# Other orders, another split between VectorE and ScalarE, and routing in steps of eight, in a fused attention and expert kernel

## The chip, the core and the metric

The kernel runs on one core of a Trainium2 chip. Its engines work from queues of their own and meet at semaphores: TensorE (PE; its weight loads are PEld), VectorE (DVE), ScalarE (ACT), GpSimd (POOL), and SyncE (SP), which issues most DMAs. The metric is the device time in microseconds (us) of one execution. An execution also comes with the clock that TensorE was granted.

## The reference

A block of 16 sequences of 512 tokens, 128 features wide. Layer-normed tokens go through an attention of 16 heads of 64 and, apart from that, through a mixture of 8 experts, of which a router picks 2 for each token. Everything is float32.

```
xn = layernorm(x)                              # x: 16 x 512 x 128
h = rmsnorm(xn) * norm_scale
q, k, v = h @ wq, h @ wk, h @ wv               # 16 heads of 64
attn = (softmax(q k^T / 8) v) @ w_out + b_out
logits = silu(xn @ rw1 + rb1) @ rw2 + rb2      # 128 -> 512 -> 8
p, e = softmax of the top 2 of logits, and which they are
ffn = sum over the 2 of p * (silu(xn @ w1[e] + b1[e]) @ w2[e] + b2[e])
out = x + attn + ffn
```

## The kernel before

The program is written out by hand as one list per engine. The work is cut into 256 steps (`group(G)`, G from 0 to 255; the sequence is `b = G // 16`, and `g = G % 16` the step in it), and six more that drain it. Two steps make a pair of heads `n = G // 2`: an even step and an odd one.

What a step of attention holds. It makes the scores of two of the pair's four row blocks (`scores`, S0 and S1, line 396, two PSUM banks each). VectorE takes the negated maxima (`maxima`, line 405) and ScalarE the exponentials (`probs`, line 411, four a step). It transposes the probabilities of the step before (`turn_probs`, T0 and T1, line 426, two banks each), and ScalarE or VectorE copies them out of PSUM (lines 438 and 441: `TURN_ON`, by row block, says who). It projects keys or queries of the next pair ("kq", `project`, line 240; ScalarE rounds them at 380, VectorE makes the rest at 381). An odd step ends with `weighted` (line 455, 16 matmuls, and OT on VectorE at 461). Steps with `g % 4 == 2` add `project_out` (lines 501 and 503), and steps with `g` in 0, 4, 8 and 12 make two value tiles (`values`; `VALUES_ON` says who copies them out, lines 361 and 363).

What goes beside it. First comes the router, in blocks of seven steps, one block for each sequence (`route`; `h = G % 7` is the step in the block). At `h` 0 and 2 `router` does two of four chunks each: 3 matmuls, two ScalarE activations (557, 560) and two POOL operations. `logits` is at 5 and `turn_logits` at 6. In the next block's `h` 0, `choose` picks the two experts in some 20 small VectorE operations, each waiting for the last (parts 0, 1 and 2: lines 615 to 620, 622 to 628, 632 to 635), with a tanh on ScalarE (629) that waits for line 628. `place` at `h` 1 works out where the tokens go, and `scatter` writes them to `slots` in HBM from POOL. After the last block `counting` writes the padding (`pads`) and has SP fetch the first rows.

Then come the experts, as 39 tiles of 512 token rows, one every three steps from step FIRST = 126 (`PLAN`: the keys are steps from `FIRST + 3 * i`). For a tile: `fetch_rows` (716) has SP load its rows, `turn_rows` transposes them (line 745) and splits them (ScalarE 750, VectorE 751); `expert_in` (h) does four chunks of 3 matmuls, each followed by two ScalarE activations (763, 765); `expert_halves` combines them on VectorE (774), rounds the sum (`HIGH_ON`, by chunk: ScalarE 777 or VectorE 779) and makes the rest on POOL (780). `expert_out` (y) does 12 matmuls (788 to 790) and ScalarE adds the bias (794); `give_back` transposes (803) and scales (807); `add_rows` has POOL add the rows to the output with four indirect DMAs (815), each lot after the landing of the lot before. Before the core ends, `again` loads the last sequence's rows from the output once all expert rows are added, and `finish` adds the last attention sum (527) and stores it (531).

What sets the order. Within a step, PE goes through the parts in the order of `PE_ORDER` (row 0 for even steps, row 1 for odd). VectorE and ScalarE sort what the step gave them by `DVE_ORDER` and `ACT_ORDER` (lines 36 to 43), where work without a place of its own is "side". POOL and SP take it as it comes. In an even step turn0 and turn1 are the copies of row blocks 2 and 3, in an odd step those of 0 and 1. All engines work in order, so an instruction that waits holds up everything behind it on its engine.

The eight PSUM banks are handed out while the list is written, by a small model with a work time and a hold time for each kind (`HOLD`, `take`): each request gets the bank that the model expects to be free first. The matmuls then wait for the operation that really empties that bank.

## Time and profile before

| | |
|---|---|
| median of 3 runs | 2053.0 us (2047.12, 2053.0, 2056.13) |
| the profiled execution's own time | 2047.12 us |
| its span, first to last instruction | 2045.3 us |
| mean granted clock | 0.989 |
| PE, PEld busy | 1955.3 us (96%), 1257.6 us (61%) |
| DVE, ACT, POOL busy | 1624.6 us (79%), 1506.4 us (74%), 930.1 us (45%) |

PE is busy 96% of the span, but matmuls are pipelined and their ends modelled, so this is no measure of how full it is. The row of starts tells more: back to back, a matmul of 512 columns starts 0.23 us after the last. The other engines have idle time on the average. Averages hide that the program has two long stages of equal step count, routing and experts, and what they are bound by has to be read stage by stage.

### The profile page before, as it was taken

To read this page: it belongs to the slowest core of one execution; us is meant where nothing else is said; L and a number is where in the kernel's file an instruction comes from. 1 tells how busy PE (TensorE), PEld (TensorE's weight loads), DVE (VectorE), ACT (ScalarE), POOL (GpSimd) and SP (SyncE) were. 2 spreads that over 40 slices of the span, in tenths; PEclk is the share of its full clock that TensorE was granted. 3 is DMA by queue.
4 is the path that set the end of the run, shared out by engine and by line. 5 is a ranking of instruction groups with operands and counts; after the bars stand their busy time and mean duration, and the time that the engine had idled before them with its cause. 6 is when DMAs were issued, how large, how long until landed. Compare 5 with 4: busy or idle time off the path is not lost.

```text
span 2045.3 us, 45195 instructions
## 1 busy us (share of the span) xinstructions
PE 1955.3 (96%) x16646; PEld 1257.6 (61%) x16646; DVE 1624.6 (79%) x2798; ACT 1506.4 (74%) x3572; POOL 930.1 (45%) x794
## 2 busy tenths in 40 slices
PE   7999999989999999989999999999999999999998
PEld 5656555556555555556666666666666666666664
DVE  7878788888888887877777777777777877777786
ACT  5767676767666666656878788888787888887865
POOL 4435364654444444310364554644645546446430
PEclk9999999999999999999999999999999999999999
DMA  2113222321111111113243333433433434334220
GB/s 84 36 56 105 80 93 75 107 77 40 40 38 38 38 43 33 34 48 93 71 79 92 80 79 89 85 85 79 84 86 79 88 81 89 88 79 84 58 37 28
DMA packets 132761, 142.22 MB, mean 70 GB/s; under 512 B 25486, under 2 KB 99086, under 8 KB 132494
## 3 DMA queue, kind: packets, MB, share of 16 engines
q1 hardware_dynamic: 101374, 118.34, 18.4%
q0 software_dynamic: 31168, 20.99, 9.0%
q8 instruction: 134, 2.20, 0.5%
q14 instruction: 85, 0.70, 0.1%
HBM read 102.92 MB, written 38.72 MB: 69 GB/s over the span
## 4 chain that ended last, share of the span: by engine, by line
PE 72%; DVE 11%; ACT 9%; issue 4%; POOL 1%; DMA 1%; another core or an unknown queue 0%; SPq 0%; DVEq 0%; ACTq 0%; POOLq 0%
PE pair L455 20%; PE pair L396 15%; PE pair L426 10%; PE pair L240 6%; PE pair L242 4%; PE pair L241 4%; DVE NM L405 4%; ACT PR L411 3%; PE pair L501 2%; PE pair L503 2%; DVE PT L441 2%; PE pair L788 1%; PE pair L790 1%; PE pair L789 1%; ACT ZT L763 1%
## 5 line engine op out<-in xcount | busy, mean ns | idle before, releaser
L411 ACT ACTIVATE PR<-pair,NM 128x512 f32<-128x512 f32 x1024 | 710.9, 717 | 30.6 <-DVE NM L405 28.0
L405 DVE TENSOR_REDUCE NM<-pair 128x2 f32<-128x1024 f32 x512 | 611.5, 1210 | 44.8 <-PE pair L396 34.8
L438 ACT COPY PT<-pair 128x512 f32<-128x512 f32 x512 | 277.2, 599 | 396.4 <-PE pair L426 395.8
L396 PE MATMUL pair<-KS,QS 64*128 64x512 f32 x3072 | 489.2, 422 | 25.9 <-ACT HS L560 10.3
L455 PE MATMUL pair<-PT,V 128*64 128x512 f32 x2048 | 474.6, 606 | 2.1 <-ACT PR L411 2.0
L426 PEld LDWEIGHTS pair<-idn,PR 64*128 64x128 f32 x8192 | 336.9, 139 | 103.9 <-ACT HS L560 22.8
L780 POOL TENSOR_TENSOR HH<-ZZ,HH 128x512 fp32r<-128x512 f32 x156 | 201.4, 1355 | 413.6 <-ACT HH L777 413.6
L396 PEld LDWEIGHTS pair<-KS,QS 64*128 64x128 f32 x3072 | 256.0, 187 | 194.2 <-issue 141.5
L426 PE MATMUL pair<-idn,PR 64*128 64x64 f32 x8192 | 343.5, 223 | 21.4 <-ACT HS L560 16.4
L441 DVE COPY PT<-pair 128x512 f32<-128x512 f32 x512 | 327.1, 680 | 8.0 <-remote 5.1
L455 PEld LDWEIGHTS pair<-PT,V 128*64 128x64 f32 x2048 | 137.1, 138 | 263.0 <-issue 248.5
L815 POOL DMA_INDIRECT out<-YS,IDW x156 | 250.1, 1603 | 60.8 <-issue 42.0
L411 ACT ACTIVATION_READ_ACCUMULATOR PR<-pair,NM 128x1 f32 x1024 | 237.7, 232 | 0.0
L461 DVE TENSOR_TENSOR OT<-pair,RB 128x512 f32<-128x512 f32 x128 | 88.4, 691 | 164.9 <-PE pair L455 160.4
L563 POOL TENSOR_TENSOR TH<-TH,HS 128x512 f32<-128x512 f32 x64 | 81.9, 1280 | 265.8 <-ACT HS L560 265.7
L774 DVE SCALAR_TENSOR_TENSOR ZZ<-ZT,ZZ 128x512 f32<-128x512 f32 x156 | 112.2, 721 | 92.2 <-ACT ZZ L765 92.2
L666 POOL DMA_INDIRECT slots<-XR,IDX x128 | 125.7, 982 | 84.6 <-DVE junk L662 53.9
L763 ACT ACTIVATE ZT<-pair,BT 128x512 f32<-128x512 f32 x156 | 114.7, 735 | 2.5 <-DVE ZZ L774 1.3
L765 ACT ACTIVATE ZZ<-pair,BT 128x512 f32<-128x512 f32 x156 | 115.6, 741 | 0.0
L381 DVE TENSOR_TENSOR QS<-pair,QS 128x512 fp32r<-128x512 f32 x128 | 87.3, 682 | 15.4 <-ACT QS L380 15.1
L381 DVE TENSOR_TENSOR KS<-pair,KS 128x512 fp32r<-128x512 f32 x128 | 87.3, 682 | 8.9 <-ACT KS L380 8.9
L777 ACT CAST HH<-ZZ 128x512 fp32r<-128x512 f32 x117 | 71.5, 674 | 23.9 <-DVE ZZ L774 23.9
(168 smaller groups left out, 2831.6 us busy)
## 6 DMA issues: line engine op xcount, KB each, us to landing
E<-w_tab SPq DMA_DIRECT2D x78, 512.0 KB
RB<-l_rows SPq DMA_DIRECT2D x127, 256.0 KB
XG<-slots SPq DMA_DIRECT2D x39, 264.0 KB
w_tab<-SPL SPq DMA_DIRECT2D x16, 512.0 KB
l_rows<-RT SPq DMA_DIRECT2D x508, 1.0 KB
xin<-in_x SPq DMA_DIRECT2D x16, 256.0 KB, 7.7
XQ<-in_x SPq DMA_DIRECT2D x16, 256.0 KB, 7.4
RAW<-in_w SPq DMA_DIRECT2D x16, 256.0 KB
```

The lines of the kernel that those rows point to most:

```text
L381: add("dve", lambda e: e.tensor_tensor(lo, bank[bk], hi, ALU.subtract), needs=[(name + "hi", n), *old], name=(name + "lo", n), place="low")
L396: m = e.matmul(bank[bk + j], a[half[j], cols], c[half[j], :], start=(k == 0), stop=(k == 2))
L405: add("dve", lambda e: e.tensor_reduce(NM[:, 2 * t:2 * t + 2], both[:], AX.X, ALU.max, negate=True), needs=[("S", n, t), *([("exp", n - 1, ...
L411: add("act", lambda e: e.activation(PR[:, k, :], bank[bk], ACT.Exp, bias=NM[:, k:k + 1], accum_out=RS[:, n % 2, j, t:t + 1]), needs=[("max ...
L426: m = e.transpose(bank[two[r]][:, at:at + DH], PR[rows, 2 * t + j, c * P:(c + 1) * P], idn[rows, rows])
L438: add("act", lambda e, r=r: e.copy(dst[r], src[r]), needs=[("T", n, t), *old], name=("PT", n, t, r), place=f"turn{t % 2}")
L441: add("dve", lambda e, r=r: e.tensor_copy(dst[r], src[r]), needs=[("T", n, t), *old], name=("PT", n, t, r), place=f"turn{t % 2}")
L455: m = e.matmul(bank[bk][j * DH:(j + 1) * DH, :], V[:, k, h * DH:(h + 1) * DH], PT[:, n % 2 * 2 + j, k, :], start=(k == 0), stop=(k == QT - 1))
L666: add("pool", lambda e, k=k, t=t: e.indirect_dma_start(slots, bass.IndirectOffsetOnAxis(ap=IDX[:, r % 2, k, t:t + 1], axis=0), XR[:, r % 2 ...
L763: add("act", lambda e: e.activation(ZT[:, n % 2], bank[bk], ACT.Tanh, bias=BT[:, i % 2, 8 + c:9 + c], scale=0.5), needs=[("h1", i, c), ("b ...
L780: add("pool", lambda e: e.tensor_tensor(lo, ZZ[:, r], hi, ALU.subtract), needs=[("hi", n), old], name=("lo", n))
L815: add("pool", lambda e, t=t: e.indirect_dma_start(out, bass.IndirectOffsetOnAxis(ap=IDW[:, i % 4, t, 0:1].bitcast(U32), axis=0), YS[:, i % ...
```

## The change

It moves work in the three tables that say who does what: one copy of row block 1's transposed probabilities a pair goes from VectorE to ScalarE (`TURN_ON`), two value copies a sequence too (`VALUES_ON`), and the rounding of expert chunks 0 and 1 goes from ScalarE to VectorE (`HIGH_ON`). The routing block gets eight steps in place of seven, so that `h` 0 is always an even step; `choose` part 0 moves to `h` 7 of the block before, and `turn_x` to `h` 7. The experts start at step 138 in place of 126. In `PLAN` the rows are fetched 2 steps before their transposes in place of 5, the transposes stand in the step of the tile before and ahead of its matmuls, and the last chunk's halves come a step earlier; the last tile hands back its rows two steps earlier than the others. The order tables and the bank model's hold times are other ones. Much of the order tables is without effect: `weighted` does nothing in even steps, `sums` and `values` have nothing in odd ones.

```diff
 PE_ORDER = [
-    "S0 weighted T0 S1 T1 kq spread attend inverse experts ahead route".split(),
-    "ahead S0 T0 S1 spread T1 kq route attend experts inverse weighted".split(),
+    "S0 T0 S1 T1 inverse kq spread attend ahead weighted experts route".split(),
+    "S0 T0 S1 spread T1 kq ahead attend experts route inverse weighted".split(),
 ]
 DVE_ORDER = [
-    "inverse max0 max1 turn1 turn0 low values sums side".split(),
-    "sums values max0 max1 turn1 low turn0 side inverse".split(),
+    "inverse max0 turn0 max1 turn1 low values sums side".split(),
+    "max0 turn0 max1 inverse turn1 sums values low side".split(),
 ]
 ACT_ORDER = [
-    "turn0 exp00 exp01 turn1 high exp10 exp11 values side hi".split(),
-    "turn0 exp00 exp01 high turn1 values exp10 exp11 side hi".split(),
+    "turn0 exp00 exp01 turn1 high exp10 exp11 values hi side".split(),
+    "turn0 exp00 exp01 high values turn1 exp10 exp11 hi side".split(),
 ]
-TURN_ON = [["act", "act"], ["dve", "dve"], ["act", "act"], ["dve", "dve"]]
-VALUES_ON = [["dve", "act", "dve", "act"], ["act", "dve", "act", "dve"]]
-HIGH_ON = ["act", "act", "dve", "act"]
+TURN_ON = [["act", "act"], ["dve", "act"], ["act", "act"], ["dve", "dve"]]
+VALUES_ON = [["dve", "act", "act", "act"], ["dve", "act", "act", "act"]]
+HIGH_ON = ["dve", "dve", "dve", "act"]
 PLAN = {
-    -7: [("rows",)],
-    -3: [("in",)],
-    -2: [("turn",)],
-    0: [("h", 0), ("halves", 0), ("h", 1), ("halves", 1), ("h", 2), ("halves", 2), ("out",), ("h", 3)],
-    2: [("halves", 3)],
+    -5: [("rows",)],
+    -3: [("turn",), ("in",)],
+    0: [("out",), ("h", 0), ("halves", 0), ("h", 1), ("halves", 1), ("h", 2), ("halves", 2), ("h", 3)],
+    1: [("halves", 3)],
     3: [("y",)],
     5: [("back",), ("add", 0), ("add", 1)],
 }
-OWN = {0: {-1: [("turn",)]}}
+OWN = {0: {-1: [("turn",)]}, -1: {2: [("y",)], 3: [("back",), ("add", 0), ("add", 1)]}}
 HOLD = {
-    "S0": (0.9, 5.2), "S1": (0.7, 6.5), "T": (0.5, 3.1), "kq": (0.8, 1.5), "V": (0.8, 2.2), "PV": (3.6, 1.4),
+    "S0": (0.9, 4.6), "S1": (0.7, 6.2), "T": (0.5, 2.5), "kq": (0.8, 1.8), "V": (0.8, 2.2), "PV": (3.6, 1.7),
...
-    ROUTE = 7
-    EARLY = ROUTE * NB // GB
-    FIRST = ROUTE * NB + 14
+    EARLY = NB // 2
+    FIRST = EARLY * GB + 10
...
         def route(G):
-            r, h = divmod(G, ROUTE)
+            r, h = divmod(G, 8)
             if 0 < r <= NB:
                 if h == 0:
-                    choose(r - 1, 0)
                     choose(r - 1, 1)
                     choose(r - 1, 2)
                 if h == 1:
                     place(r - 1)
-                if 2 <= h <= 4:
+                if r == NB:
+                    if h == 2:
+                        scatter(r - 1, slice(0, 8))
+                elif 2 <= h <= 4:
                     scatter(r - 1, slice(3 * h - 6, 3 * h - 3))
...
+            if h == 7:
+                choose(r, 0)
             if r + 1 < NB:
...
-                if h == 6:
+                if h == 7:
                     turn_x(r + 1)
 
         def counting(G):
-            k = G - ROUTE * NB
+            k = G - 8 * NB
             if k == 2:
                 totals()
-            if 6 <= k < 10:
-                pads(2 * k - 12)
-                pads(2 * k - 11)
-            if k == 7:
+            if 4 <= k < 8:
+                pads(2 * k - 8)
+                pads(2 * k - 7)
+            if k == 5:
                 fetch_weights(0, 0)
+            if k == 6:
+                fetch_weights(0, 1)
             if k == 8:
-                fetch_weights(0, 1)
-            if k == 10:
                 fetch_rows(0)
                 fetch_rows(1)
```

The first place is VectorE's queue where the router's choice stands. In the kernel before, this is the end of an even step at `h` 0: KS is the key rest, acc the output sum, gm and gt hold the choice.

```order
L381 TENSOR_TENSOR KS<-pair1,KS 128x512 [waits s_act_khi]
L510 TENSOR_TENSOR acc<-pair3,acc 128x512 [waits s_dve_acc,s_pe_OP]
L615 TENSOR_REDUCE gm<-LG 128x4 [waits s_dve_gate]
L616 TENSOR_TENSOR gt<-LG,gm 128x32 [waits s_dve_gate]
L617 SCALAR_TENSOR_TENSOR gt<-gt,CON 128x32 [waits s_dve_gate]
L618 TENSOR_REDUCE gm<-gt 128x4 [waits s_dve_gate]
L619 TENSOR_TENSOR gt<-CON,gm 128x32 [waits s_dve_gate]
L620 SCALAR_TENSOR_TENSOR gt<-gt,LG 128x32 [waits s_dve_gate]
```

Thirteen more small operations of `choose` follow, and then the next step's first maxima. In the changed kernel part 0 stands at the end of the odd step before (lines after the edit are two lower):

```order
L379 TENSOR_TENSOR QS<-pair0,QS 128x512 [waits s_act_qhi]
L613 TENSOR_REDUCE gm<-LG 128x4 [waits s_dve_gate]
L614 TENSOR_TENSOR gt<-LG,gm 128x32 [waits s_dve_gate]
L615 SCALAR_TENSOR_TENSOR gt<-gt,CON 128x32 [waits s_dve_gate]
L616 TENSOR_REDUCE gm<-gt 128x4 [waits s_dve_gate]
L617 TENSOR_TENSOR gt<-CON,gm 128x32 [waits s_dve_gate]
L618 SCALAR_TENSOR_TENSOR gt<-gt,LG 128x32 [waits s_dve_gate]
L344 TENSOR_TENSOR XT<-pair3,XT 128x512 [waits s_pe_r1,s_act_xTs]
L459 TENSOR_TENSOR OT<-pair1,RB 128x512 [waits s_RB_0,s_pe_PV]
L464 RECIPROCAL RI<-RS 128x8 [waits s_dve_rt,s_act_exp]
L467 STREAM_TRANSPOSE RT<-RI 128x32 [waits s_rrow_1,s_dve_ri]
L403 TENSOR_REDUCE NM<-pair0 128x2 [waits s_pe_S]
```

and parts 1 and 2 stay at the end of the even step, ahead of the next step's first maxima (NM):

```order
L379 TENSOR_TENSOR KS<-pair1,KS 128x512 [waits s_act_khi]
L620 TENSOR_REDUCE gm<-gt 128x4 [waits s_dve_gate]
L621 TENSOR_TENSOR gt<-gt,gm 128x32 [waits s_dve_gate]
L622 SCALAR_TENSOR_TENSOR gt<-gt,CON 128x32 [waits s_dve_gate]
L623 TENSOR_REDUCE gm<-gt 128x4 [waits s_dve_gate]
L624 TENSOR_TENSOR gt<-CON,gm 128x32 [waits s_dve_gate]
L625 TENSOR_TENSOR gt<-gt 128x32 [waits s_dve_gate]
L626 TENSOR_TENSOR gm<-gm 128x4 [waits s_dve_gate]
L630 TENSOR_TENSOR PM<-PM,gt 128x8 [waits s_dve_pm] x4
L633 COPY PM<-PM 128x8 [waits s_dve_pm]
L403 TENSOR_REDUCE NM<-pair1 128x2 [waits s_pe_S]
```

Six of the operations have moved one step ahead; the others still stand before the maxima.

The second place is ScalarE's queue in an even step that carries an expert tile's matmuls. The kernel before (V is a value copy, ZT and ZZ the activations of the four chunks, YT the bias of the tile before, HH the rounding, PT the next step's first copies; pair0 to pair3 are the bank pairs):

```order
L361 COPY V<-pair2 128x512 [waits s_pe_V]
L763 ACTIVATE ZT<-pair3,BT 128x512 [waits s_bt_0,s_pe_h1]
L765 ACTIVATE ZZ<-pair3,BT 128x512 [waits s_pool_lo]
L763 ACTIVATE ZT<-pair0,BT 128x512 [waits s_pe_h1]
L765 ACTIVATE ZZ<-pair0,BT 128x512 [waits s_pool_lo]
L763 ACTIVATE ZT<-pair2,BT 128x512 [waits s_dve_s,s_pe_h1]
L765 ACTIVATE ZZ<-pair2,BT 128x512 [waits s_pool_lo]
L763 ACTIVATE ZT<-pair0,BT 128x512 [waits s_dve_s,s_pe_h1]
L765 ACTIVATE ZZ<-pair0,BT 128x512 [waits s_pool_lo]
L794 ACTIVATE YT<-pair2,BT 128x512 [waits s_pe_yT,s_pe_w2]
L777 CAST HH<-ZZ 128x512 x2
L438 COPY PT<-pair3 128x8x64 [waits s_pe_PV,s_pe_T]
```

The changed kernel, in the same place:

```order
L359 COPY V<-pair3 128x512 [waits s_pe_V]
L748 CAST X2<-pair3 128x512 [waits s_pe_h1,s_pe_xg]
L761 ACTIVATE ZT<-pair0,BT 128x512 [waits s_bt_0]
L763 ACTIVATE ZZ<-pair0,BT 128x512 [waits s_pool_lo]
L761 ACTIVATE ZT<-pair1,BT 128x512
L763 ACTIVATE ZZ<-pair1,BT 128x512 [waits s_pool_lo]
L761 ACTIVATE ZT<-pair1,BT 128x512 [waits s_dve_s]
L763 ACTIVATE ZZ<-pair1,BT 128x512 [waits s_pool_lo]
L761 ACTIVATE ZT<-pair0,BT 128x512 [waits s_dve_s]
L763 ACTIVATE ZZ<-pair0,BT 128x512 [waits s_pool_lo]
L792 ACTIVATE YT<-pair3,BT 128x512 [waits s_pe_yT,s_pe_w2]
L436 COPY PT<-pair3 128x8x64 [waits s_pe_PV,s_pe_T]
```

The cast of the next tile's rows (X2), which waits for the last `expert_in` matmul (s_pe_h1), now stands ahead of all eight activations, and the two roundings behind them are gone.

On PE, this is what follows the tile's last `expert_out` matmul in such a step (E2 is the second weight, PR the probabilities). It reads like this in both kernels; only the second signal that T0's bank waits for differs:

```order
L788 MATMUL pair2<-HH,E2 128x512
L394 MATMUL pair3<-KS,QS 128x512 [waits s_act_exp]
L394 MATMUL pair3<-KS,QS 128x512 x5
L424 MATMUL pair1<-idn,PR 128x64 [waits s_act_zz,s_dve_xl]
L424 MATMUL pair1<-idn,PR 128x64 x15
L394 MATMUL pair0<-KS,QS 128x512 [waits s_act_zz]
L394 MATMUL pair0<-KS,QS 128x512 x5
L424 MATMUL pair2<-idn,PR 128x64 [waits s_act_ye]
L424 MATMUL pair2<-idn,PR 128x64 x15
```

The second transposes T1 (the last two rows) go into the bank that YT empties (s_act_ye).

The third place is VectorE's queue in such a step. Before:

```order
L381 TENSOR_TENSOR KS<-pair3,KS 128x512 [waits s_act_khi]
L510 TENSOR_TENSOR acc<-pair0,acc 128x512 [waits s_dve_acc,s_pe_OP]
L774 SCALAR_TENSOR_TENSOR ZZ<-ZT,ZZ 128x512 [waits s_act_zz,s_act_zt] x3
L779 CAST HH<-ZZ 128x512 [waits s_pe_w2,s_dve_s]
L405 TENSOR_REDUCE NM<-pair2 128x2 [waits s_pe_S]
L405 TENSOR_REDUCE NM<-pair3 128x2 [waits s_pe_S]
L441 COPY PT<-pair1 128x8x64 [waits s_pe_T]
```

and after the change:

```order
L379 TENSOR_TENSOR KS<-pair1,KS 128x512 [waits s_act_khi]
L749 TENSOR_TENSOR X2<-pair3,X2 128x512 [waits s_pe_h1,s_act_xh]
L772 SCALAR_TENSOR_TENSOR ZZ<-ZT,ZZ 128x512 [waits s_act_zz,s_act_zt]
L777 CAST HH<-ZZ 128x512 [waits s_pe_w2,s_dve_s]
L772 SCALAR_TENSOR_TENSOR ZZ<-ZT,ZZ 128x512 [waits s_act_zz,s_act_zt]
L777 CAST HH<-ZZ 128x512 [waits s_dve_s]
L772 SCALAR_TENSOR_TENSOR ZZ<-ZT,ZZ 128x512 [waits s_act_zz,s_act_zt]
L777 CAST HH<-ZZ 128x512 [waits s_dve_s]
L403 TENSOR_REDUCE NM<-pair2 128x2 [waits s_pe_S]
```

The three sums (ZZ) stood together with one rounding behind them; now each has its rounding (HH) behind it, and X2 stands ahead, all before the next step's maxima.

## Rows read from the trace of the kernel before

**Rows 1.** Stretches, routing then experts: length, busy PE, PEld, DVE, ACT, POOL, clock, DMA, GB/s.
```profile
16.70:861.90 845.20, 789.23 (x6950) 488.72 (x6950) 695.84 (x1420) 583.87 (x1438) 395.80 (x375) 0.98 0.17 57
...
979.80:1924.90 945.10, 936.13 (x7682) 623.83 (x7680) 737.18 (x1065) 764.12 (x1742) 484.62 (x372) 1.00 0.38 83
```
**Rows 2.** The first stretch, line 396 alone: length, PE, PEld, clock, DMA, GB/s.
```profile
16.70:861.90 845.20, 213.47 (x1344) 111.24 (x1344) 0.98 0.17 57
```
**Rows 3.** Timeline of three late steps: start, length, engine, instruction.
```profile
1996.50 0.96 PE L396 MATMUL pair<-KS,QS 64*128 64x512 f32 x6
...
2001.73 0.96 PE L396 MATMUL pair<-KS,QS 64*128 64x512 f32 x6
...
2008.83 0.96 PE L396 MATMUL pair<-KS,QS 64*128 64x512 f32 x6
```
**Rows 4.** Timeline of step 43, odd, at h 1, and its neighbours.
```profile
338.42 0.18 DVE L615 TENSOR_REDUCE gm<-LG 128x4 f32<-128x32 f32 x1
...
339.09 0.96 PE L396 MATMUL pair<-KS,QS 64*128 64x512 f32 x6
...
342.38 0.20 ACT L629 ACTIVATE gm<-gm 128x4 f32<-128x4 f32 x1 [3.66 <-DVE gm L628]
...
345.04 1.12 PE L426 MATMUL pair<-idn,PR 64*128 64x64 f32 x16 [3.75 <-ACT HS L560]
...
352.78 0.97 PE L396 MATMUL pair<-KS,QS 64*128 64x512 f32 x6
```
**Rows 5.** The costliest copies, from the page's groups: busy, mean ns.
```profile
L438 ACT COPY PT<-pair 128x512 f32<-128x512 f32 x512 | 277.2, 599 | 396.4 <-PE pair L426 395.8
...
L441 DVE COPY PT<-pair 128x512 f32<-128x512 f32 x512 | 327.1, 680 | 8.0 <-remote 5.1
```
**Rows 6.** Timeline of step 174, even, with an expert tile, on PE and ACT.
```profile
1374.79 0.39 PE L242 MATMUL pair<-X,E 128*128 128x512 f32 x1
...
1377.59 0.40 PE L790 MATMUL pair<-HH,E 128*128 128x512 f32 x1
1377.92 0.96 PE L396 MATMUL pair<-KS,QS 64*128 64x512 f32 x6
...
1379.96 0.65 PE L426 MATMUL pair<-idn,PR 64*128 64x64 f32 x16
```
**Rows 7.** The same step's activations on ACT, first and last.
```profile
1373.13 0.69 ACT L763 ACTIVATE ZT<-pair,BT 128x512 f32<-128x512 f32 x1
...
1377.13 0.73 ACT L765 ACTIVATE ZZ<-pair,BT 128x512 f32<-128x512 f32 x1
```
**Rows 8.** Lines 774 and 779 alone: shortest, median and longest ns.
```profile
L774 DVE SCALAR_TENSOR_TENSOR ZZ<-ZT,ZZ x156: 677/692/1725, 969.9 to 1948.9; 128x512 f32<-128x512 f32 x156
...
L779 DVE CAST HH<-ZZ x39: 426/428/703, 973.0 to 1935.9; 128x512 fp32r<-128x512 f32 x39
```
**Rows 9.** Timeline of step 150, DVE and POOL: three sums beside POOL's work.
```profile
1171.21 3.48 DVE L774 SCALAR_TENSOR_TENSOR ZZ<-ZT,ZZ 128x512 f32<-128x512 f32 x3 [1.23 <-ACT ZZ L765]
1171.83 1.71 POOL L780 TENSOR_TENSOR HH<-ZZ,HH 128x512 fp32r<-128x512 f32 x1
```
**Rows 10.** Timelines before the first expert tile: SP issue, POOL's first use, PE's first.
```profile
943.76 1.61 SPq L716 DMA_DIRECT2D XG<-slots  x2
...
950.57 0.19 POOL L754 COPY IDW<-XG 128x8 f32<-128x8 f32 x1 [61.19 <-DMA XG<-slots]
...
958.40 0.60 PE L745 MATMUL pair<-idn,XG 128*128 128x128 f32 x4
```
**Rows 11.** The last steps' timeline: the reload of the last rows, the last addition.
```profile
2024.06 0.43 SPq L1017 DMA_DIRECT2D xin<-out  x1
...
2041.44 0.69 DVE L527 TENSOR_TENSOR xin<-pair,xin 128x512 f32<-128x512 f32 x1 [0.75 <-PE pair L519]
```
**Rows 12.** DMA issues by line: size, us from issue to landing.
```profile
xin<-out SPq DMA_DIRECT2D x1, 256.0 KB, 7.6
```
**Rows 13.** Line 815 alone, the indirect adds: shortest, median, longest ns.
```profile
L815 POOL DMA_INDIRECT out<-YS,IDW x156: 1546/1562/2045, 1011.7 to 1989.3; - x156
```

4 rows, old and new, of the table HOLD are left out of this document.

## Prediction

> **What bounds the kernel now.** I read the busy time by stretch first, because averages over the span mix two stages. Steps 0 to 111 take 845.2 us (7.55 a step) and steps 128 to 239 take 945.1 (8.44) [rows 1]; each holds 112 steps, 1344 score matmuls at twelve a step [rows 2]. In the expert stretch PE is busy 936.1 of 945.1 us at a granted clock of 1.00, in the routing stretch 789.2 of 845.2 at 0.98. So the expert stage is full of matmuls, and a wait there adds to the time almost one for one, while there is nothing to win. The routing stage has 56 us without a matmul, which is all that an edit can win.
>
> The timeline says where these 56 us lie. Attention alone makes a pair of steps in 12.33 us (1996.50 to 2008.83), 5.23 even and 7.10 odd [rows 3]. Step 43, odd and at `h` 1, takes 13.69 us (339.09 to 352.78) [rows 4]. There `choose` holds up VectorE from 338.42, ScalarE's tanh waits 3.66 for its line 628, the router's activations stand behind the tanh, and the T1 transposes wait 3.75 for the bank that the router's HS (line 560) empties. With blocks of seven, `h` 1 is odd in every second block.
>
> **A, the routing stage.** An odd step with router work and without a stall I put at 7.7 (7.10 and 0.6 for the router's matmuls), so the stall of step 43 is 6.0. Seven such steps lie in the stage; 37 us (5.3 each, a little under step 43, since 7 x 6.0 = 42 would leave too little of the 56 for the rest) is what they can give. With blocks of eight, `h` 0 is always even and `choose` in all 16 blocks stands before an odd step. Six of its 20 operations move to the odd step before. Up to line 628 there are 13, which took 3.96 (338.42 to 342.38, [rows 4]), 0.30 each; without six the tanh comes 1.8 sooner. So the wait is about halved and not gone: ScalarE's tanh, the activations behind it and with them T1's bank still come late. VectorE also loses a copy of 680 ns a pair [rows 5]. Of the 3.75 that T1 waited [rows 4], 1.8 and 0.7 go, which leaves 1.3 in each of 16 odd steps, 21 us. A = -37 + 21 = -16. Bounds: -37 if the shorter `choose` is hidden; +5 if the copy doesn't help, because ScalarE now makes it (599 ns [rows 5]) just ahead of the late activations, and 2.6 a block remain (3.75 - 1.8 + 0.6; 16 x 2.6 = 42).
>
> **B, the expert stage.** The rows of PE in the change show that T1 goes into the bank of YT. Now the X2 cast, which waits for the tile's last `expert_in` matmul, stands ahead of all eight activations. In step 174 that matmul starts at 1374.79 and ends at 1375.18, the last of `expert_out` ends at 1377.99, and T1 starts at 1379.96 [rows 6]. The eight activations started at 1373.13, the last at 1377.13, 0.57 apart [rows 7]: they ran beside the matmuls, and YT was due when `expert_out` ended. In the new order the same step runs so: the cast starts at about 1375.3 and takes some 0.6, the eight activations end at 1375.9 + 8 x 0.57 + 0.15 = 1380.6, YT at about 1381.1. T1, wanted at 1379.96, waits 1.1. Of the 39 tiles 20 start in an even step; in 19 of these T1 has this bank.
>
> VectorE comes on top. Its three sums now wait for activations that are done later, each with a rounding of 0.43 behind it in place of one for all [rows 8], and POOL's line 780 (1.71) falls between them. Beside POOL's work the sum of 692 ns grew to as much as 1725 [rows 8]; in step 150 three of them took 3.48 in place of 2.1 [rows 9]. The Trainium skill, "SBUF — State Buffer", section "Who interferes with whom", says that a VectorE operation with two inputs in SBUF, or a copy or cast in a two-port mode, excludes a GpSimd operation that uses the shared pair for as long as either runs. The trace agrees as far as the sums go (1725 against 692), and by that rule the roundings would be drawn in as well. The longest rounding of before took 703 against 428 [rows 8]. With the last sum due at 1380.6 at the earliest and 0.69 + 0.43 behind it, the next step's maxima start near 1383 and not near 1381, and exponentials and the odd step's banks follow. I put this at 0 to 0.9 more. Per even tile 1.1 to 2.0, and 1.4 as my value, nearer to 1.1, because that end stands on rows alone: 20 x 1.4 = 28 us.
>
> In the 19 odd tile steps the 16 matmuls of `weighted` (3.65 us or so) follow the expert matmuls and hide most of it; there I put 0.2 each, 4 us. B = +32. Bounds: +5, if ScalarE makes up for the cast in the slack between YT and T1 (1.4 us in rows 6, from 1377.99 plus YT's 0.6 to 1379.96), and +60 at 2.6 an even tile and 0.4 an odd one.
>
> **C, the changeover.** SP fetched the first rows at 943.76, POOL used them at 950.57, and PE at 958.40 [rows 10], a slack of 7.83 us. PE now uses them one step after the fetch and not three, so two steps (a pair, 12.33) are gone: 12.3 - 7.8 = 4.5, and PE waits about 5 us, once. Bounds 0 and 8. In later tiles the fetch is 2 steps, near 17 us, before the transposes; the first one needed 6.8 from issue to use (943.76 to 950.57), so these cost nothing. C = +5.
>
> **D, the tail.** Before, the last rows were reloaded at 2024.06, and the last sum started at 2041.44 [rows 11]; the reload takes 7.6 [rows 12], so it was 9.8 early. The four adds of the last tile now come in step 255, which starts near 2026.4 (2008.83 + 12.33 + 5.23, [rows 3]). From about 2027 they take 6.2 to issue (4 x 1.56, [rows 13]) and two landings, for which no row stands and I allow 2 each; the reload then starts at 2037.5 and lands at 2045, 4 late, and I take 5 with the hand-back before them. Bounds 0 and +12.
>
> The moves of equal price (the order tables' other entries, `turn_x` at `h` 7, the split of VectorE's and ScalarE's copies outside the places above) I put at nothing: what hides them is the idle time of VectorE and ScalarE in the expert stretch (945.1 less 737 and less 764, [rows 1]). With that cover gone they would cost what B's upper bound holds.
>
> **The sum.** -16 + 32 + 5 + 5 = +26. The profiled execution took 2047.1 in all; that makes 2073. The median of the three is 5.9 above it. I take half of that, and come to 2076. What can be told from no change is 0.5%, about 10 us to either side of 2053 (2043 to 2063).
>
> **The rivals.**
> *R1, the orders do little (near 2053).* T1's wait in the even tile steps is 1.1 or less with no part of VectorE's, and the routing stage gives 25: -25 + 15 + 10 = 0 from 2053. For it: DVE and ACT are busy at most 81% of the expert stretch [rows 1], and lateness of one step can be made up for in the next two. Against it: a wait of PE in a stage in which PE is 99% busy isn't made up for.
> *R2, faster (near 2025).* The routing stalls go entirely (-37), the clock there rises from 0.98 to 1.00 with them, and YT comes before T1; with 10 for C and D that is 2026. It decides at the point where YT ends against T1's start: if the activations of chunks 0 to 2 get ahead of the cast's wait, or `expert_in` ends 1.1 us earlier in the step, nothing is left of B. For it: 56 us are there. Against it: the order of the rows of ScalarE.
> *R3, slower by much (near 2095).* PE's pauses in the expert stage bring its clock down, as in the routing stage, where the mean granted clock is 0.98 with stalls of this kind and 1.00 without them [rows 1]. 2% of 945 is 19 us more: 2076 + 19 = 2095. The Trainium skill, "TensorE: Matmul & The Clock Gate", section "A second HAM failure mode: psum-queue depth-cycling", describes a kernel whose small idle times between groups of matmuls, cycling through PSUM banks, made the clock swing between its levels. Here the stage with the short waits alone shows 1.00, and only the one with stalls of several us shows less, which speaks for the rule's effect only if the new waits are longer than 1 to 2 us.
>
> **Chances.** The forecast 0.50, of which 0.03 lies within 0.5%; R1 0.20 (0.12 same, 0.04 slower, 0.04 faster); R3 0.16, slower; R2 0.14, faster. Together slower 0.67, same 0.15, faster 0.18. The forecast's own range is 2060 to 2092. The range for 8 in 10 leaves R2's core out, and reaches over R1 and most of R3: 2038 to 2110, which also holds the sum with B at 5 (2049) and at 60 (2104).
>
> **What would show it.** A: in the routing stage, waits of T1 (now line 424) on HS in all odd steps after `choose`, about 1.3 and not 3.75, and the stage's steps at 7.4 (7.55 before). B: in even tile steps ScalarE idle before the X2 cast, T1 waiting about 1 us for YT some 19 times, lines 772 and 777 longer than 692 and 428 ns, steps at 8.7 (8.44 before). C: one wait of PE on XG of about 5. D: a sum at the end that waits for the reload. I am wrong if T1 doesn't wait for YT, or if the expert stage still takes 8.44 a step.

## The result and the profile after

The changed kernel took 2102.1 us (median of four, 2101.68 to 2103.31) against 2052.9 (2047.12 to 2056.13): 1.0244 of the time before, 95% interval 1.0221 to 1.0267. That is 49 us slower where 23 were forecast (2076 against 2053). Its profiled execution took 2104.14 with a span of 2102.3, 57 us over the span of before, of which the forecast's sum had explained 26.

Stretches of the changed kernel: steps 0 to 111, the changeover 128 to 137, the expert steps 138 to 254 (columns as in [rows 1]).

```profile
17.10:829.00 811.90, 767.45 (x6892) 475.66 (x6892) 643.94 (x1285) 604.32 (x1489) 354.57 (x337) 1.00 0.18 57
...
948.00:1033.65 85.65, 69.58 (x596) 43.53 (x594) 55.37 (x103) 48.46 (x122) 10.13 (x12) 0.88 0.24 70
...
1033.65:2074.30 1040.65, 990.90 (x8006) 655.76 (x8004) 819.03 (x1114) 793.29 (x1813) 519.71 (x381) 0.99 0.35 77
```

Steps 0 to 111 fell from 845.2 to 811.9, partly because they hold 14 routing blocks and no longer 16. The expert steps take 8.89 each and PE has 50 us without a matmul in these 117 steps, where it had 9 in the 112 steps of 945.1 us [rows 1]. To compare kernels whose stages have other lengths, I take step starts from the starts of the first score matmul, and from each stage the attention alone, 6.17 us a step (half of 12.33, [rows 3]). What is left is the stage's excess. Routing is steps 0 to 111 (before) or 0 to 127 (changed), the gap reaches from there to the first tile, and the experts' column begins with the first tile and ends 120 steps later, which is when the last tile's rows go back, or at step 255 where the core's steps end sooner (117 steps, in the runs with the changed routing). The tiles are means over tiles 2 to 35:

| run, with its edit | routing | gap to the first tile | experts | from step 255's start | even tile, odd tile (3 steps) |
|---|---|---|---|---|---|
| before | 154 | 14 | 269 | 20.7 | 24.29, 26.53 |
| changed | 141 | 24 | 319 | 28.0 | 26.07, 27.29 |
| e5 before, X2 ahead | 137* | 12 | 315 | 22.4 | 26.34, 26.78 |
| e6 before, chunks 0, 1 on VectorE | 137* | 11 | 331 | 20.7 | 27.02, 27.10 |
| e10 before, chunk 0 | 154 | 17 | 305 | 20.7 | 26.14, 26.63 |
| e11 before, chunk 1 | 155 | 16 | 268 | 22.3 | 24.20, 26.57 |
| e14 before, last halves earlier | 162 | 16 | 294 | 20.7 | 24.85, 27.31 |
| e1 changed, X2 back | 139 | 23 | 364 | 27.7 | 27.40, 28.65 |
| e2 changed, roundings back | 139 | 22 | 320 | 27.0 | 26.47, 26.85 |
| e3 changed, hold times back | 137 | 25 | 318 | 27.6 | 26.06, 27.22 |
| e4 changed, splits back | 150 | 22 | 321 | 26.9 | 26.16, 27.31 |
| e9 changed, X2 and roundings back | 137 | 24 | 305 | 27.1 | 24.79, 27.93 |
| e15 as e9, order tables back | 137 | 24 | 308 | 27.2 | 24.99, 27.99 |
| e13 as e9, whole plan back | 135 | 21 | 270 | 30.6 | 24.43, 26.70 |
| e7 before, routing changed | 120* | 20 | 259 | 30.9 | 24.10, 26.51 |
| e8 before, part 0 earlier | 111* | 10 | 267 | 22.4 | 24.18, 26.54 |
| e12 before, parts 0, 1 earlier | 159 | 15 | 270 | 20.7 | 24.30, 26.52 |
| e16 as e8, splits changed | 138 | 14 | 275 | 20.7 | 24.43, 26.70 |
| e17 as e8, tanh behind router | 144* | 9 | 267 | 22.4 | 24.18, 26.53 |

The starred runs come from two groups of runs in which the kernel before took 2027 and 2028 us and not 2051 to 2054; its untouched routing stage had 137 there (e5, e6) and not 154 (e10, e11). Ratios are always against before in the same group, and routing excesses are compared only within one group. So the change's 57 us by stage: routing -13, changeover +10, experts +50, the end +7, and +3 because the nine steps after the last tile, which had 3 less than the 6.17, are gone. Over the same 117 steps from the first tile the experts' excess rose from 264 to 319, by 55; before, the last tile's second matmuls and hand-back came in the three steps behind these, and 5 of the 269 with them.

The granted clock moves between stages. The trace has TensorE at its lower level (0.50, 1.2 GHz) for 37.5 us of the routing stage before and for 10.2 after, for 6.8 and 20.5 us of the changeover, and for 0 and 13.7 us of the same 117 expert steps. As the level is half of the other one, such a stretch can cost at most half its length. So the clock gave up to 14 us back in the routing stage, and took up to 7 in each of the other two.

PE's waits in the expert stage, changed kernel (total us, times, longest):

```profile
PE pair L424 <- ACT YT L792: 11.8, 15, 1.1
PE pair L394 <- DVE KS L379: 9.7, 10, 1.2
PE pair L394 <- ACT ZZ L763: 7.2, 5, 2.0
PE pair L453 <- ACT PR L409: 5.2, 4, 1.3
PE pair L424 <- DVE OT L459: 5.0, 3, 2.1
```

and of before, which had next to none:

```profile
PE pair L788 <- POOL HH L780: 3.5, 2, 1.8
PE pair L240 <- ACT PT L438: 3.1, 9, 0.7
PE pair L426 <- ACT PT L438: 1.8, 3, 0.6
```

Step 186 of the changed kernel, even, with a tile (the place of [rows 6, 7]):

```profile
1470.34 0.39 PE L240 MATMUL pair<-X,E 128*128 128x512 f32 x1
...
1470.82 0.59 ACT L748 CAST X<-pair 128x512 fp32r<-128x512 f32 x1 [2.90 <-PE pair L240]
1471.30 0.70 ACT L761 ACTIVATE ZT<-pair,BT 128x512 f32<-128x512 f32 x1
...
1474.15 1.65 POOL L778 TENSOR_TENSOR HH<-ZZ,HH 128x512 fp32r<-128x512 f32 x1 [4.91 <-DVE HH L777]
...
1474.70 1.39 DVE L777 CAST HH<-ZZ 128x512 fp32r<-128x512 f32 x1
...
1475.87 0.74 ACT L792 ACTIVATE YT<-pair,BT 128x512 f32<-128x512 f32 x1
...
1476.76 0.71 PE L424 MATMUL pair<-idn,PR 64*128 64x64 f32 x16 [0.77 <-ACT YT L792]
```

ScalarE stands idle for 2.90 until the last `expert_in` matmul, casts X2, and only then begins the eight activations, 0.57 apart; T1 waits for YT. A rounding beside POOL's subtraction takes 1.39 and not the 0.43 of [rows 8]. The changeover and the end:

```profile
1027.24 1.12 PE L743 MATMUL pair<-idn,XG 128*128 128x128 f32 x4 [4.88 <-DMA XG<-slots]
...
2091.41 0.66 PE L517 MATMUL pair<-idn,acc 128*128 128x128 f32 x4 [0.79 <-DVE acc L508]
2094.44 0.42 SPq L1019 DMA_DIRECT2D xin<-out  x1
2097.41 0.69 DVE L525 TENSOR_TENSOR xin<-pair,xin 128x512 f32<-128x512 f32 x1 [6.06 <-DMA xin<-out]
```

The last sum waits for the reload, 5.3 us after its transposes end (2092.07); before, the reload was issued 17 us ahead of the sum [rows 11].

### The profile page after: what moved, and what is told of

The parts are those of the page before. It is cut to its first block, busy times and chain, and to the rows that moved or that the text cites. A ratio compares the mean times of both kernels' runs of the same rounds, so it can differ in the third digit from the quotient of the medians.

```text
span 2102.3 us, 45192 instructions
## 1 busy us (share of the span) xinstructions
PE 1966.5 (94%) x16646; PEld 1261.2 (60%) x16646; DVE 1627.6 (77%) x2716; ACT 1541.4 (73%) x3654; POOL 945.3 (45%) x790
## 4 chain that ended last, share of the span: by engine, by line
PE 65%; ACT 13%; DVE 11%; issue 7%; DMA 1%; another core or an unknown queue 1%; POOL 0%; SPq 0%; DVEq 0%; POOLq 0%; ACTq 0%
PE pair L453 17%; PE pair L394 12%; PE pair L424 9%; PE pair L238 6%; PE pair L240 5%; PE pair L239 4%; ACT PR L409 4%; DVE NM L403 4%; DVE ZZ L772 2%; PE pair L499 2%; PE pair L501 2%; ACT PT L436 2%; ACT ZZ L763 1%; ACT HS L558 1%; DVE PT L439 1%
## 5 line engine op out<-in xcount | busy, mean ns | idle before, releaser
L436 ACT COPY PT<-pair 128x512 f32<-128x512 f32 x640 | 360.1, 612 | 362.7 <-PE pair L424 362.5
L424 PE MATMUL pair<-idn,PR 64*128 64x64 f32 x8192 | 345.9, 223 | 41.9 <-ACT HS L558 18.1
L778 POOL TENSOR_TENSOR HH<-ZZ,HH 128x512 fp32r<-128x512 f32 x156 | 225.9, 1490 | 325.2 <-DVE HH L777 168.3
L813 POOL DMA_INDIRECT out<-YS,IDW x156 | 244.6, 1568 | 176.1 <-DVE YS L805 118.7
L439 DVE COPY PT<-pair 128x512 f32<-128x512 f32 x384 | 251.1, 682 | 21.9 <-remote 16.4
L772 DVE SCALAR_TENSOR_TENSOR ZZ<-ZT,ZZ 128x512 f32<-128x512 f32 x156 | 120.0, 769 | 23.3 <-ACT ZZ L763 23.3
L777 DVE CAST HH<-ZZ 128x512 fp32r<-128x512 f32 x117 | 111.8, 955 | 13.1 <-PE pair L788 10.3
L749 DVE TENSOR_TENSOR X<-pair,X 128x512 fp32r<-128x512 f32 x39 | 27.0, 692 | 111.0 <-ACT X L748 107.6
```

The source lines that it names most:

```text
L424: m = e.transpose(bank[two[r]][:, at:at + DH], PR[rows, 2 * t + j, c * P:(c + 1) * P], idn[rows, rows])
L436: add("act", lambda e, r=r: e.copy(dst[r], src[r]), needs=[("T", n, t), *old], name=("PT", n, t, r), place=f"turn{t % 2}")
L439: add("dve", lambda e, r=r: e.tensor_copy(dst[r], src[r]), needs=[("T", n, t), *old], name=("PT", n, t, r), place=f"turn{t % 2}")
L772: add("dve", lambda e: e.scalar_tensor_tensor(ZZ[:, r], ZT[:, n % 2], 1.0, ZZ[:, r], ALU.add, ALU.mult), needs=[("zt", n), ("zz", n)], nam ...
L778: add("pool", lambda e: e.tensor_tensor(lo, ZZ[:, r], hi, ALU.subtract), needs=[("hi", n), old], name=("lo", n))
L813: add("pool", lambda e, t=t: e.indirect_dma_start(out, bass.IndirectOffsetOnAxis(ap=IDW[:, i % 4, t, 0:1].bitcast(U32), axis=0), YS[:, i % ...
```

## The experiments

**e1_turn**, the changed kernel with this entry of the plan set back (and `side` ahead of `hi` in `ACT_ORDER`, as in e2, e9, e13 and e15):

```diff
-    -3: [("turn",), ("in",)],
+    -3: [("in",)],
+    -2: [("turn",)],
```

> The changed kernel with one entry of its plan set back: the next tile's rows are transposed and split (X2) one step after the expert matmuls and not in their step ahead of them, so ScalarE's cast no longer stands ahead of the eight activations. The order table has the late roundings behind the side work again, which by itself moves nothing. Theory 1 (the cast makes the activations, YT and with it T1 late, and this is most of what the expert stage lost): the wait of T1 on YT, 1 us in the even tile steps, goes, the expert stage falls from 8.90 us a step to at most 8.6 and the time from 2102 to 2075 or less. Theory 2 (VectorE's three roundings beside POOL's work are most of it): 2092 to 2102, the waits on VectorE's KS and OT stay. Theory 3 (which bank each request gets is most of it): no firm number, since the banks are drawn anew, but the waits on ACT YT turn into waits on other signals of the same length, near 2095.

Measured 1.0453 (1.0432 to 1.0475), 45 us slower than the changed kernel. All three theories miss it. The waits on YT are nearly gone, but T1's place is taken by others: the scores wait 17.8 us for ZZ, and T1 16.6 for the copies. Something else makes ScalarE late when the cast doesn't.

**e2_high**: `HIGH_ON` back to act, act, dve, act.

> The changed kernel with the roundings of expert chunks 0 and 1 back on ScalarE (the order table as in the run beside it; by itself it moves nothing). Theory 1 (the cast ahead of the activations): nothing gained, 2095 to 2110, since ScalarE gets 1.2 us more a tile behind late activations. Theory 2 (roundings on VectorE, which POOL's port stretches from 0.43 to 0.95 us each): VectorE is 2 us a tile less busy, the waits of PE on KS, OT and on maxima go, and the time falls to 2080 or less. Theory 3 (banks): the banks are the same, so within 5 us of 2102.

1.0240 (1.0219 to 1.0261): no change, as theory 1 has it. While the cast is ahead, the roundings on VectorE cost nothing, stretched as they are.

**e3_hold**: the `HOLD` table of before.

> The changed kernel with the bank model's hold times of the kernel before, nothing else. Theories 1 and 2: every engine's queue but the choice of banks is the same, so the late activations and roundings stay and the time is 2095 to 2110. Theory 3 (the choice of banks is most of the loss): 2080 or less, with the waits of T1 on YT gone.

1.0212 (1.0195 to 1.0229), expert excess 318. The waits turn from YT to ZZ, and PE's time without a matmul stays (50 us, then 53). The bank model's hold times aren't the cause. Other hold times change only which bank each request gets, so that choice is tried as far as these two sets of times differ.

**e4_split**: `TURN_ON` and `VALUES_ON` of before.

> The changed kernel with the split of the probability copies and of the value copies between ScalarE and VectorE of before (one copy a pair and two value copies a sequence back on VectorE). Theory 1: ScalarE has 0.6 us a pair less in front of it, but VectorE 0.7 more; in the expert stage within 0.05 us a step, in the routing stage the choice comes 0.7 later, 16 x 0.3 = 5 us more: 2100 to 2110. Theory 2 (VectorE is what is late in the expert stage): 0.7 us more VectorE a pair beside the roundings costs 0.1 to 0.3 a step there, 2112 to 2130.

1.0311 (1.0293 to 1.0328). The new split was the one good part of these edits, worth 0.7%, in the profiled executions 9 us in the routing stage and 2 in the experts'. The time lies in theory 2's range, but not where that puts it; theory 1 had the place right and half the size.

**e5_b_turn**, the kernel before with the inverse of e1:

> The kernel before with one edit: the next tile's rows are transposed and split (X2) in the step of the tile before, ahead of its matmuls, so ScalarE's cast stands ahead of the eight activations. Theory 1 (the cast alone makes the expert stage slower): YT and T1 late in even tile steps as in the changed kernel, 20 x 1.1 to 1.8 us, 2053 becomes 2075 to 2090. Theory 2 (the roundings on VectorE are needed for it): within 10 us of 2053. Theory 3 (banks): anything between, with waits on other signals than YT.

1.0224 (1.0207 to 1.0241). This one line in the kernel before costs 46 us of expert excess, nearly all that the whole change lost there, 2.05 in each even tile. That is theory 1's cause, and more than its 1.8 a tile; but T1 waits for YT only 3.3 us in all, and S1 for the bank of ZZ 16.4, which was theory 3's sign. In both cases the bank comes free late because ScalarE's activations are late.

**e6_b_high**, the kernel before with `HIGH_ON` dve, dve, dve, act:

> The kernel before with one edit: expert chunks 0 and 1 are rounded on VectorE as well. Theory 1: VectorE has slack in the expert stage (633 us busy of 812), so within 10 us of 2053. Theory 2 (the roundings beside POOL's work on VectorE): the roundings take about 0.9 us each in place of 0.43, the maxima behind them come 1.8 later, and the time is 2070 to 2090.

1.0309 (1.0292 to 1.0326), 62 us of excess, more than either theory allows. Its step 174 shows a wait that I hadn't priced:

```profile
1381.42 0.43 DVE L779 CAST HH<-ZZ 128x512 fp32r<-128x512 f32 x1 [2.91 <-PE pair L790]
...
1382.48 1.37 DVE L779 CAST HH<-ZZ 128x512 fp32r<-128x512 f32 x1
1382.54 0.69 ACT L763 ACTIVATE ZT<-pair,BT 128x512 f32<-128x512 f32 x1 [2.52 <-DVE ZZ L774]
...
1384.53 0.96 PE L396 MATMUL pair<-KS,QS 64*128 64x512 f32 x6 [1.83 <-ACT YT L794]
```

The first rounding writes the buffer that the tile before is still being multiplied from, so it waits 2.91 for the last `expert_out` matmul. Behind it in VectorE's queue is the second sum, and chunk 3's tanh waits for that, 2.52. So the rounding makes the last activations as late as the cast does, by another way.

**e10_high_c0** and **e11_high_c1**, chunk 0 alone (dve, act, dve, act) and chunk 1 alone (act, dve, dve, act):

> The kernel before with chunk 0 alone rounded on VectorE besides chunk 2. The rounding stands behind the first sum and waits for the last expert_out matmul (its buffer's last reader), so the second sum and with it chunk 3's tanh wait. Theory 1 (this wait in VectorE's row is the cost): nearly the whole loss of the run with chunks 0 and 1, 1.024 to 1.03 of the time before. Theory 2 (the roundings beside POOL's subtractions on the shared port are the cost): half of that, 1.01 to 1.017.

> The kernel before with chunk 1 alone rounded on VectorE besides chunk 2: as many roundings beside POOL's work as in the run with chunk 0, but it stands behind the second sum, so chunk 3's tanh, which needs that sum, is free. Theory 1 (the wait that holds the second sum is the cost): ScalarE isn't held, only VectorE's third sum and the maxima are 1 us later: 1.000 to 1.008. Theory 2 (the port): as with chunk 0, 1.01 to 1.017.

1.0166 (1.0149 to 1.0183), and 1.0004 (0.9991 to 1.0017). The same operation, the same number of times, costs 36 us ahead of the second sum and nothing behind it. e10 lies in the range that I had given to the port, but its roundings aren't stretched (the median is 0.43 in both runs), and in e10 those of chunk 0 wait 81 us in all, ahead of the second sum. Those of chunk 1 in e11 wait 38 us, but behind the second sum, and no activation stands behind them. So the cost is the wait in that place. Both roundings together cost 26 more than chunk 0 alone; there those of chunks 1 and 2 take 1.37 and 1.39 (medians) beside POOL's subtractions:

```profile
L779 DVE CAST HH<-ZZ x117: 426/1372/1400, 950.4 to 1979.3; 128x512 fp32r<-128x512 f32 x117
```

```profile
L779 DVE CAST HH<-ZZ x78: 426/427/746, 974.4 to 1938.0; 128x512 fp32r<-128x512 f32 x78
```

(e6, then e11.) That the port is what these 26 are was not tried apart.

**e9_turn_high**: e1 and e2 together.

> The changed kernel with both edits set back: X2 is made a step after the expert matmuls, and chunks 0 and 1 are rounded on ScalarE. Theory 1 (the cast ahead of the activations, and the first rounding's wait on VectorE for the second matmuls of the tile before, each make the last activations about 2.5 us late in even tile steps, and together no later than one alone): only with both gone does the expert stage recover, from 8.89 us a step to 8.45 to 8.55, and the time is 1.000 to 1.006 of the kernel before. Theory 2 (orders, the rest of the plan, banks carry half of the loss): 8.7 a step, 1.012 or more.

1.0170 (1.0153 to 1.0187). Even tiles recover to 24.79, as theory 1 has it; odd tiles don't, at 27.93, so the time is theory 2's: another part of the change is at work. Of the 50 us, 36 are still there (305 against 269). With the cast back, the roundings on VectorE cost 59 (e1 against this run).

**e14_b_h3**, the kernel before with the last chunk's sum, rounding and rest a step earlier:

```diff
-    2: [("halves", 3)],
+    1: [("halves", 3)],
```

> The kernel before with one edit: the last chunk's sum, rounding and rest come one step after the tile's first step and not two. Theory 1: in odd tiles they then stand at the end of an even step, just ahead of the copies and maxima of the odd one, and ScalarE's rounding waits for VectorE's sum: 0.8 to 1.4 us in each of 19 odd tiles, 1.007 to 1.014. Theory 2 (this edit costs only beside the changed order tables): 0.997 to 1.003.

1.0099 (1.0074 to 1.0125): 24 us of expert excess, 0.78 an odd tile and 0.56 an even one. The 0.56 is nearly all in two even tiles (8 and 24), 3.8 us longer each: T1 waits 3.1 and 3.0 us for OT there, and as the wait ends TensorE falls to its lower level for 6.8 us. One of the two, then the stretch of low clock (columns as in [rows 1]):

```profile
1200.02 1.12 PE L426 MATMUL pair<-idn,PR 64*128 64x64 f32 x16 [3.10 <-DVE OT L461]
```

```profile
1199.60:1206.30 6.70, 6.28 (x31) 4.88 (x33) 5.45 (x10) 5.10 (x13) 1.28 (x1) 0.50 0.08 23
```

The odd tiles are regular. PE's wait and its cause in step 167:

```profile
1328.76 0.69 DVE L751 TENSOR_TENSOR X<-pair,X 128x512 fp32r<-128x512 f32 x1 [0.30 <-ACT X L750]
...
1329.37 0.91 DVE L774 SCALAR_TENSOR_TENSOR ZZ<-ZT,ZZ 128x512 f32<-128x512 f32 x1
...
1330.31 0.62 ACT L777 CAST HH<-ZZ 128x512 fp32r<-128x512 f32 x1 [1.58 <-DVE ZZ L774]
1330.84 1.07 ACT L438 COPY PT<-pair 128x512 f32<-128x512 f32 x2
...
1331.47 0.50 PE L240 MATMUL pair<-HT,WQ 128*128 128x512 f32 x1 [0.73 <-ACT PT L438]
```

The sum stands behind X2's rest, ScalarE holds the rounding 1.58 for it, and the copies that free the banks stand behind the rounding.

**e13_plan** and **e15_orders**: e9 with the whole plan of before, and e9 with its order tables.

> The changed kernel with ScalarE's roundings and the whole expert plan of before (the last chunk's halves two steps after the tile's first and not one, rows fetched five steps ahead); orders, splits, bank model and routing are the changed ones. With the transposes and roundings alone set back, even tiles recovered (24.8 us in three steps, 24.3 before) and odd ones did not (27.9 against 26.5), with PE waiting for ScalarE's copies behind the last chunk's rounding. Theory 1 (the last chunk's halves a step earlier): odd tiles fall to 26.5 to 26.8 and the time to 1.000 to 1.006 of before. Theory 2 (order tables or banks): odd tiles stay at 27.5 or more, 1.012 to 1.017.

> The changed kernel with X2, the roundings and the three order tables of before; the rest of the changed plan stays, with the last chunk's halves a step earlier. Theory 1 (that step is what odd tiles lose): 1.012 to 1.019, as without the tables. Theory 2 (the tables): odd tiles at 26.5 to 26.8, 1.000 to 1.006.

1.0008 (0.9999 to 1.0018), expert excess 270; and 1.0147 (1.0125 to 1.0170), excess 308. Setting back the plan and the roundings takes away 49 of the changed kernel's 319, setting back the order tables nothing. The plan was set back as a whole: beyond e9 that gives 35, where the halves alone cost 24 in the kernel before (e14). The halves alone were not tried in that kernel, so how much of the 35 is theirs, and how much comes from `out` ahead of the chunks, the later fetch or the splits beside them, stays open. e7 below has the same plan and blocks with the splits, tables and hold times of before, and 259 where e13 has 270.

**e7_b_route8** and **e8_b_choose**: before with the routing, changeover and first tile of the changed kernel; and before with the one edit

```diff
                 if h == 0:
-                    choose(r - 1, 0)
...
             if h == 6:
                 turn_logits(r)
+                choose(r, 0)
```

> The kernel before with the routing of the changed kernel and nothing else: blocks of eight steps, part 0 of the choice a step earlier, the scatter of the last block in one step, the experts from step 138. The routing stage should give 13 us (the excess over plain attention steps was 154 before and 141 in the changed kernel), the changeover should cost 10 (wait for the first rows, clock), the last tile's adds and the reload 7 to 10 at the end. Sum +4 to +7: 2053 to 2062. If the orders and splits of the changed kernel are needed for the routing gain, it is 2065 or more; if the end and the changeover cost less with the plan of before, 2045 or less.

> The kernel before with one edit: part 0 of the choice (six small VectorE operations) moves from the first step of a routing block to the last step of the block before. If the stall at the steps at h 1 is the length of the choice ahead of the maxima (13.7 us in step 43, where a step without it takes 7.7), 1.8 us go in each of the seven odd ones, 10 to 15 us in all: 2038 to 2043. If the stall is set by something else (the clock, the scatter, the tanh), within 5 us of 2053.

0.9991 (0.9981 to 1.0000) and 0.9889 (0.9872 to 0.9905). Blocks of eight together with part 0 give 17 us of routing and pay for it in the gap (8) and at the end (10); of the 10 in the experts' column 5 are the three steps that it has less. Part 0 alone gives 26 us of routing, twice what I expected: odd steps at `h` 1 fall from 13.4 (e5, e6; 13.1 in before) to 10.0. The stage in e5, whose routing is that of before, and in e8 (columns as in [rows 1]):

```profile
17.13:845.13 828.00, 789.58 (x6950) 489.98 (x6950) 694.36 (x1420) 584.58 (x1438) 395.67 (x375) 0.97 0.18 58
```

```profile
16.65:818.75 802.10, 774.92 (x6950) 482.84 (x6950) 695.43 (x1426) 586.04 (x1438) 396.18 (x375) 0.99 0.18 60
```

PE's time without a matmul falls from 38 to 27 us, by the 10 to 15 that I expected. The other 15 are matmul time: the same 6950 matmuls are busy 790 us and then 775, as TensorE is at its lower level for 44 us in e5 and 10 in e8. **e18_choose_again** repeated it:

> The kernel before with part 0 of the choice a step earlier, a second time, beside the run above on the same chip: 0.987 to 0.991 again if its gain doesn't depend on the chip, nearer to 0.994 if part of it came from the chip that ran it first, on which the kernel before took 2026.8 us.

0.9885 (0.9868 to 0.9902), again in a group where before took 2028. It wasn't run alone where before takes 2051 to 2054; e16, part 0 with the changed splits, has 138 us of routing there against 154. It is the fastest version here, faster than both kernels.

**e12_choose01** (parts 0 and 1), **e16_choose_split** (part 0 and the changed splits), **e17_late** (part 0, and `router` listed ahead of the rest of `choose` at `h` 0):

> The kernel before with parts 0 and 1 of the choice (13 operations and the tanh) in the last step of the block before. With part 0 alone moved, the time was 0.989 of before, and in step 43 T1 still waited 2.44 us for HS, with the tanh standing 2.32 for VectorE. If the tanh's wait is what is left, T1 waits under 0.5 there and the time is 0.978 to 0.985. If the wait only moves one step ahead (ScalarE then holds the tanh in the last step of the block), it is 0.986 to 0.995.

> The kernel before with part 0 of the choice a step earlier (0.989 of before by itself) and the changed split of the probability and value copies (one copy a pair and two value copies a sequence more on ScalarE). In the changed kernel this split was worth 0.7% (9 us of it in the routing stage). If that holds here: 0.982 to 0.988. If ScalarE is what is late in the expert stage of this one, it costs there what it gives in the routing stage: 0.989 to 0.995.

> The kernel before with part 0 of the choice a step earlier, and in the block's first step the router's two chunks listed ahead of the rest of the choice, so that on ScalarE the tanh stands behind the router's four activations and no longer in front of them; PE's and VectorE's queues are those of the run with part 0 alone moved. If the tanh's wait for VectorE is what keeps HS and T1's bank late (2.44 us in step 43), that wait goes, and the time is 0.975 to 0.985 of before. If VectorE's lateness with the maxima is what is left, it is within 0.004 of the run beside it.

e12: 1.0008 (0.9996 to 1.0020), outside both ranges: the stall moves a step ahead, the odd steps at `h` 0 now take 13.0. e16: 0.9923 (0.9900 to 0.9947), the second range: the splits cost 6 to 8 us in the experts' stage here. And e17: 1.0033 (1.0022 to 1.0043), against both expectations; step 43 tells why, e17 first and then e8:

```profile
339.06 1.30 POOL L565 TENSOR_TENSOR HS<-HS,TH 128x512 f32<-128x512 f32 x1
339.14 3.82 DVE L632 TENSOR_TENSOR PM<-PM,gt 128x8 f32<-128x8 f32 x4
...
340.33 1.27 POOL L563 TENSOR_TENSOR TH<-TH,HS 128x512 f32<-128x512 f32 x1
341.67 1.27 POOL L565 TENSOR_TENSOR HS<-HS,TH 128x512 f32<-128x512 f32 x1
```

```profile
328.19 0.76 DVE L632 TENSOR_TENSOR PM<-PM,gt 128x8 f32<-128x8 f32 x4
```

With the tanh behind the router's activations, POOL's operations on their results (1.3 each) start while VectorE is still in the choice, and four additions of eight columns take 3.82 and not 0.76. In the whole of e17, 22 of the 64 such additions take over 0.6 us, each while POOL works; in e8 and e18 none does.

## Why the prediction was wrong

**B, the expert stage, is the step that failed:** 32 were forecast, 50 came (55 over equal steps), within my bound of 60. Its first part held. T1 waited for YT (0.77 in step 186, up to 1.1; 1.1 was the forecast), in 15 places and not 19, and the step after an even tile's first took 8.94 in the mean and not 7.83. Even tiles lost 1.78, where I had 1.4. What was mis-sized most is the odd tiles: "there I put 0.2 each" measured 0.76. By these means the even tiles are 7 us of the 18 that B lacks, and the odd ones 11. I let `weighted` hide all that happens in them, and gave the last chunk's halves a step earlier no term at all, though the plan shows it. That edit alone costs 24 us in the kernel before (e14), about 15 of them in the odd tiles, and 36 of the changed kernel's 50 stay when only the cast and the roundings are set back (e9) and go with the rest of the plan (e13). I also read the rounding's wait for the second matmuls past, though it stands in the order's row; alone it costs 36 (e10), with the second rounding 59 in the changed kernel without the cast (e1 against e9), and beside the cast nothing (e2). The parts don't add: 46, 62 and 24 alone, 50 together, where the cast and the rounding make the same activations late. Which of them is credited with the 50 depends on the order of undoing; setting back only the cast adds 45 to the excess (e1).

**A** came near in its number and not in its mechanism, so that is luck: -16 forecast, -13 measured. PE waited 18.1 us for HS at T1 in 22 places, longest 1.3, and the forecast had 16 times 1.3; but before it was 16.4 in 16 places, longest 3.7, and 10.3 more ahead of scores. In the whole stage PE had 56 us without a matmul before and has 53 after:

```profile
17.06:948.06 931.00, 878.24 (x7880) 544.47 (x7880) 733.62 (x1461) 688.96 (x1698) 397.58 (x377) 0.99 0.17 54
```

So waiting gave 3 us, and the other 10 are matmul time, at a mean clock of 0.995 against 0.978. "All that an edit can win" was therefore not the 56 us without a matmul; of the clock's return only R2 spoke. The copy's split carries 9 of the gain (e4), and the better part of the change was the one that I had only as "six go" (e8).

**C** was right in its mechanism and half in its size: XG kept PE waiting 4.88 as worked out, and PE's time without a matmul rose by 5 in all (11 to 16), but the changeover cost 10: the granted clock over its steps was 0.88, and 0.97 before, a term that the forecast left out. **D**: the wait for the reload was 5.3, as forecast; in all the end is 7.3 longer, where I had 5. With the nine steps (3), which had no term, the parts add up: 18 from B, 3 from A, 5 from C, 2 from D and 3 are the 31 between 26 and 57.

**Orders and banks at nothing** held nearly: 3 us (e15), and 5 (e3). The splits, also held at nothing in the expert stage, cost 6 to 8 there beside the plan of before (e16), and gave 2 beside the changed one (e4). **The rivals:** R1 and R2 are out, though R2's clock is what gave A most of its gain. R3's 2095 is nearest to what came, but its clock is a small part: the expert stage has 0.99, three stretches at the lower level that can cost 7 us of the 55 and not 19. They came as R3 had it, behind waits: the one at 1165.0 began 1.2 us after a wait of 2.09, and the falls of e5 (3.4 us at a time) came behind waits of 1.26 followed by 0.54. The rule on the shared port ("SBUF — State Buffer", "Who interferes with whom" in the Trainium skill) says that a cast in a two-port mode is blocked while GpSimd has the shared pair; the 1.39 us rounding beside POOL's 1.65 fits it. By it I leaned to the port as the second cost in even tiles; the runs give the wait for `expert_out` that place.

**The reference of the sum:** the profiled execution of before was the fastest of its four, 5.8 under the median, and that of the changed kernel 2 over its own. That is 8 of the 57, of which the forecast took 3 into account.

## What to carry to other kernels

In an engine that works in order, ask of each moved instruction what it waits for, not how long it takes: here a cast of 0.6 us and a rounding of 0.43 us cost 46 and 36 us because of what stood behind them, and the same rounding one place later cost nothing. When several edits make the same late thing late, undo them together as well as one by one; each alone looks like all of the loss or like none. And a wait costs more than its length when the granted clock falls behind it: ask of a stage not only where PE stands idle, but what its matmuls would take at the full clock. A split of a serial chain over two steps (six of twenty operations a step earlier) was worth more than moving more of it.

## What the hardware showed

The tanh that held ScalarE for 2.3 us had kept POOL from VectorE's way: putting it behind the router's activations cost 1.4% against the same kernel in the same group (e17 against e18), because small VectorE operations of 0.17 us took up to 1.27 us beside POOL's.

Shorter stalls in the routing stage came with more time at the full clock, and with it the same 6950 matmuls were busy 15 us less (e8 against e5). In the expert stage single waits of 1.3 to 3.1 us came just ahead of stretches of 3.4 to 6.8 us at half the clock (e5, e14), while the kernel before, with next to no waits, had none in that stage.

The kernel before took 2051 to 2054 us in some groups of runs and 2027 to 2028 in others, 1.3% apart. Some 17 of these 24 us lie in the routing stage (154 against 137 us of excess), as time in which PE waits (56 against 38), in the steps at `h` 4 above all: 5.9 and 8.4 us against 5.1 and 7.4, even and odd. Two groups that differ so carry the same chip number in their results (9), so it isn't shown that the chip makes the difference; the cause stays open.
